# Four small changes of order and place in a two-layer transformer kernel: last addition, score buffer, a square root, a value tile

## The chip, the cores and the metric

The kernel runs on one core of a Trainium2 chip as one program. The metric is device time in microseconds (us). The core has a matrix engine (TensorE, PE in the profile, its weight loads PEld), VectorE (DVE), ScalarE (ACT), GpSimd (POOL) and SyncE (SP), which here only issues transfers. Each engine takes its instructions in the order of its own program and waits on semaphores that the others raise. PE writes only to PSUM (`ps`, eight banks of 128x512 numbers).

## The reference, cut to what matters

Two layers over x of 1024 tokens by 256:

```python
for each layer:
    xn = layernorm(x)
    s  = attention(xn)
    g  = silu(ffn(xn))
    x  = x + s * g
```

The second attention has 16 query heads and 4 key/value heads of width 128. It works on 1024 tokens in a causal way:

```python
scores = q @ k.T + alibi            # alibi: slope * distance
scores = 30.0 * tanh(scores / sqrt(128) / 30.0)
probs  = softmax(causal(scores));  ctx = probs @ v
```

The second ffn routes each token to 4 of 32 experts, plus one shared expert:

```python
logits = flat @ router_w.T
scores = sqrt(softplus(logits))
_, idx = top_k(scores + expert_bias, 4)
```

Precision is kept by splitting each operand of a product in a high and a low part (`_hi`, `_lo`); three matmuls (lines 516 to 518 of the profile, the helper `mm3`) make one product.

## The kernel before, in words

**Order.** All semaphores and orders are written by hand. For the second layer `schedule()` writes one list of steps, and `follow(engine)` makes from it the list of each engine. The steps are: `project(n, half)` (one q or k head for 512 tokens), `values(t)` (the value tile of 128 tokens), `scores(h, j)` (scores of head h with key tile j against all later queries, (8-j)*128 wide), `context(h, t)`, `turn` (transposing the context), `out` (projecting it), and the router's small parts. A score row has the number n = 8*h + j; this text calls it row n, and there are 128 of them. `context` of head h-1 runs beside the scores of head h. A table `ROUTER` says behind which score row each router part stands, for ACT and DVE apart; the DVE parts are numbered 0 to 9 up to the biased router score.

**A score row.** PE makes row n in one of two PSUM halves (n % 2). It waits that DVE has read row n-2 (`s1_bias`). DVE adds the distance term and writes the sum to `cap` (L1509). ACT takes tanh in place (L1160) and exp from there into `P1` (L1165), and POOL masks the diagonal tile of `P1` (L1738). `cap` has two slots of 1024, used in turn. DVE may write row n once ACT's exp of row n-2 is done (`s1_exp`).

**Start of the heads.** `project` goes PE, DVE (products with cos and sin, L1497 and L1499), POOL (their sum, L1845), ACT (the high part, L1154), POOL (the low part, L1853). Row 0 needs the low part of the second half of head 0's q. `values` is made by PE and copied from PSUM by DVE (L1480).

**Router.** sqrt(softplus) is computed with Exp, Ln and Sqrt on ACT (parts 0, 1, 2 of ACT, L1178, L1181 and L1184) and one Newton step on DVE behind each (for the square root, DVE parts 6 to 8, L1565 to L1570). ACT loads another function table when it goes from Exp or Tanh to Ln or Sqrt and back.

**End.** For each token tile t DVE adds pairs of expert rows (L1713), PE sums them (L952), ACT takes silu (L1230, `mix1_a`), DVE multiplies with `s_tok` (L1723, `mix1_b`), POOL adds the product to `x_tok` (L1882), and SP sends the tile out (L508). `mix1_a` and `mix1_b` have two slots each; DVE's loop makes the pairs of tile t and then the product of tile t-2. The names in the profile leave buffer numbers out: `P` is `P1`, `yp`/`gu` hold the pair sums, `mix_b` is `mix1_b`, `scr` is any of the router's scratch rows.

Of the kernel before, what the change touches and what calls it, by code (L numbers as in the profile page):

```python
# [7 lines left out]
ALU = mybir.AluOpType  # L8
ACT = mybir.ActivationFunctionType
# [7 lines left out]
P = 128  # L17
TOK = 1024
NT = TOK // P
# [78 lines left out]
H1, G1, D1 = 16, 4, 128  # L98
REP = H1 // G1
CAP = 30.0  # L100
# [12 lines left out]
NO_ROW = 1 << 20  # L113


OFF = [sum((NT - i) * P for i in range(j)) for j in range(NT + 1)]
TRI = OFF[NT]

# [35 lines left out]
def build_program(nc, x_in, wqkv_in, wout_in, lns_in, lnb_in, packed_in, scales_in,  # L154
# [5 lines left out]
    with ExitStack() as ctx:  # L160
        def sem(name):
            return ctx.enter_context(nc.semaphore(name))

        def alloc(scope):
            return lambda name, shape, dt=F32: scope.enter_context(nc.sbuf_tensor(name, shape, dt))


        sb = alloc(ctx)
        ident = sb("ident", [P, P])
        x_tok = sb("x_tok", [P, NT, D])  # L170
# [19 lines left out]
        sb = alloc(l0)  # L190
# [21 lines left out]
        sb = alloc(l0m)  # L212
# [14 lines left out]
        sb = alloc(l0w)  # L227
# [5 lines left out]
        sb = alloc(l0w)  # L233
# [10 lines left out]
        sb = alloc(l0a)  # L244
# [25 lines left out]
        sb = alloc(l1b)  # L270
# [16 lines left out]
        mix1_b = sb("mix1_b", [P, 2, D])  # L287
# [7 lines left out]
        sb = alloc(l1a)  # L295
# [10 lines left out]
        k_lo = sb("k_lo", [P, 2, TOK], F32R)  # L306
        P1 = sb("P1", [P, 2, TRI])
        V1 = sb("V1", [P, NT, G1, D1 + 1])
        cap = sb("cap", [P, 2, TOK])
        dist = sb("dist", [P, TOK])  # L310
        rot = sb("rot", [P, 3, HALF])
        c_rden = sb("c_rden", [P, 3, 1])
# [91 lines left out]
        fT_ready, f_ps, fth_ready, x_ready = sem("fT_ready"), sem("f_ps"), sem("fth_ready"), sem("x_ready")  # L404
        table_ready = sem("table_ready")
        mixed, shift_ready = sem("mixed"), sem("shift_ready")
# [4 lines left out]
        s1_ps, s1_bias, s1_exp, s1_mask = sem("s1_ps"), sem("s1_bias"), sem("s1_exp"), sem("s1_mask")  # L411
# [101 lines left out]
        def _(pe):  # L513
# [276 lines left out]
            def context(h, t):  # L790
# [8 lines left out]
                for j in range(t + 1):  # L799
                    a = OFF[j] + (t - j) * P  # L800
                    last = pe.matmul(ps[:, 4 + r % 2, o:o + D1 + 1], P1[:, h % 2, a:a + P], V1[:, j, h // REP, :],  # L801
# [170 lines left out]
        def _(act):  # L972
# [71 lines left out]
            for s in range(2 * U0):  # L1044
# [10 lines left out]
                t = tile_at(s, 2)  # L1055
# [11 lines left out]
            for t in range(NT + 1):  # L1067
                if 2 <= t < NT:
                    stack_hi(t)
                if t >= 1:  # L1070
                    r = t - 1
# [21 lines left out]
            for n in range(len(UNITS0)):  # L1093
                R, heads, a, e = UNITS0[n]
                w = e - a
# [60 lines left out]
            def scores(h, j):  # L1156
                n = h * NT + j
                w = (NT - j) * P
                act.wait_ge(s1_bias, n + 1)
                act.activation(cap[:, n % 2, 0:w], cap[:, n % 2, 0:w], ACT.Tanh, scale=1.0 / (CAP * float(D1) ** 0.5))\  # L1160
                    .then_inc(act_step, 1)
                act.wait_ge(act_step, n + 1)
                if j == 0 and h >= 2:
                    act.wait_ge(c_ps, 3 * (h - 1))
                act.activation(P1[:, h % 2, OFF[j]:OFF[j] + w], cap[:, n % 2, 0:w], ACT.Exp, scale=CAP)\  # L1165
                    .then_inc(s1_exp, 1)

            def turn_part(h, half):
# [65 lines left out]
        def _(dve):  # L1234
            steps = [2]
# [164 lines left out]
            for t in range(NT + 1):  # L1400
                if 2 <= t < NT:
                    stack_lo(t)
                if t >= 1:
                    r = t - 1
# [97 lines left out]
            def scores(h, j):  # L1502
                n = h * NT + j
                w = (NT - j) * P
                dve.wait_ge(s1_ps, n + 1)
                if n >= 2:
                    dve.wait_ge(s1_exp, n - 1)
                slope = float(np.float32(2.0) ** np.float32(-(h + 1) * 8.0 / H1))
                dve.scalar_tensor_tensor(out=cap[:, n % 2, 0:w], in0=dist[:, 0:w], scalar=slope,  # L1509
                                         in1=psf[:, 1024 * (n % 2):1024 * (n % 2) + w], op0=ALU.mult, op1=ALU.add)\  # L1510
                    .then_inc(s1_bias, 1)

# [202 lines left out]
            for t in range(NT + 2):  # L1715
                if t < NT:
                    add_pairs(t)
                if t >= 2:
                    r = t - 2
                    dve.wait_ge(fth_ready, r + 1)  # L1720
                    if r >= 2:
                        dve.wait_ge(x_ready, NT + r - 1)
                    dve.tensor_tensor(mix1_b[:, r % 2, :], mix1_a[:, r % 2, :], s_tok[:, r, :], ALU.mult).then_inc(mixed, 1)  # L1723


        @block.gpsimd
        def _(pool):
            steps = [0]
# [104 lines left out]
            def scores(h, j):  # L1833
                causal(P1[:, h % 2, OFF[j]:OFF[j] + P], s1_exp, h * NT + j, s1_mask)

# [41 lines left out]

            for b in range(NBLK):
                send_y(b)
            for t in range(NT):  # L1880
                pool.wait_ge(mixed, NT + t + 1)
                pool.tensor_tensor(x_tok[:, t, :], x_tok[:, t, :], mix1_b[:, t % 2, :], ALU.add).then_inc(x_ready, 1)  # L1882

VAR_STEP = 2 * NT + 1
STACK_STEPS = (2 * U0 - 5, 2 * U0 - 3)
# [2 lines left out]
TOP_PARTS = 10  # L1888
SUM_PARTS = TOP_PARTS + 5 + TOPK
PICK_PARTS = SUM_PARTS + 6  # L1890
ROUTER = {"act": [11, 14, 28],
          "dve": [12, 20, 20, 21, 22, 23, 29, 30, 31, 31]
          + [36, 37, 38, 39, 44, 44, 45, 46, 47]
          + [52, 53, 54, 55, 60, 61]
          + [62, 63, 68, 69, 70, 71, 76, 77]
# [9 lines left out]
def schedule():  # L1905

    steps = []
    first = PROJ.index(("q", 0))
    steps += [("project", 0, 0), ("values", 0), ("values", 1), ("turn_x", 1, 1), ("project", first, 0), ("values", 2), ("values", 3)]
    steps += [("project", 0, 1), ("project", first, 1)] + [("values", t) for t in range(4, NT)]  # L1910
    for h in range(H1 + 1):

        todo = []
        if h + 1 < H1:
            at = PROJ.index(("q", h + 1))
            if h % REP == 2 and h // REP + 1 < G1:
                todo += [("project", at - 1, 1)]
            todo += [("project", at, 0), ("project", at, 1)]
            if h % REP == 1 and h // REP + 1 < G1:
                todo += [("project", at + 1, 0)]  # L1920
        if h == 0:
            todo += [("logits", 0, 0), ("logits", 0, 1), ("turn_logits", 0, 0)]
        for j in range(NT):
            if h < H1:
                steps.append(("scores", h, j))
            if h >= 1:
                steps.append(("context", h - 1, j))

            outs = [("out", (h - 2) // PAIR - 1, 1 + 2 * j + i) for i in (0, 1) if 1 + 2 * j + i < NT]
            outs = outs if h >= PAIR + 2 and (h - 2) % PAIR == 0 else []  # L1930
            steps += outs[:1]
            if todo:
                steps.append(todo.pop(0))
            steps += outs[1:]

            if h >= 2 and j in (3, 4):
                steps.append(("turn", h - 2, j - 3))
            if h >= PAIR + 1 and (h - 2) % PAIR == PAIR - 1 and j == 7:
                steps += [("out", (h - 2) // PAIR, 0)]
            if h == RANKS_AT and j == 3:  # L1940
                steps.append(("ranks", 0, 0))
    steps += [("turn", H1 - 1, 0), ("turn", H1 - 1, 1)]
    steps += [("moe", s) for s in range(MOE_EARLY)]
    return steps
# [8 lines left out]
def follow(engine):  # L1953
# [3 lines left out]
    for n, s in enumerate(STEPS1):  # L1957
# [4 lines left out]
        if name == "scores":  # L1962
            out.append(s)
            if engine in ROUTER:
                out += [("router", part) for part, at in enumerate(ROUTER[engine]) if at == NT * s[1] + s[2]]
            if engine == "pool" and NT * s[1] + s[2] in SEND_AT:
# [114 lines left out]
```

## Time and profile before

| | us |
|---|---|
| median of 3 runs | 845.72 (844.31 to 847.45) |
| the profiled execution, its own time | 846.73 |
| its span in the trace | 844.9 |
| PE / PEld busy | 787.4 / 642.0 |
| DVE / ACT / POOL busy | 605.4 / 465.3 / 429.8 |

The span is 1.8 us shorter than the execution's own time; that rest lies outside the trace. A row of the timeline has the start in us from the span's start, the duration in us, the engine, the line, the operation with output and input, the shapes and the count, and in brackets how long the engine had been idle before it and which work ended that wait. A wait is put down to the work that came last, and where an instruction waits for two things the named one can be the wrong one. In the windows view PEclk is the granted clock of TensorE: 1.00 is 2.4 GHz and 0.50 is 1.2 GHz.

### The profile page before, as it was taken

The page shows a single profiled execution, that of the slowest core. Times are in us where ns is not written, and L with a number is a line of the kernel's source. Part 1 is how long each engine was busy: PE and PEld are TensorE (multiplying, and loading weights), DVE is VectorE, ACT ScalarE, POOL GpSimd, SP SyncE. Part 2 cuts the span into 40 slices and gives each one's busy share as a digit, 9 for nine tenths or more (in the row PEclk, how much of TensorE's full clock was granted, in tenths as well). Part 3 has the DMA queues.
Part 4 walks back from the last instruction along what each step waited for, and adds up shares of the span by engine and source line. Part 5 has one row for each costly group of instructions (what it writes and reads, how often), then busy time and mean ns, then how long its engine had stood idle before and what let it go on. Part 6 is the DMA issues. An engine that isn't in the chain of part 4 may idle for free.

```text
span 844.9 us, 14053 instructions
## 1 busy us (share of the span) xinstructions
PE 787.4 (93%) x4927; PEld 642.0 (76%) x4927; DVE 605.4 (72%) x1069; ACT 465.3 (55%) x822; POOL 429.8 (51%) x487
## 2 busy tenths in 40 slices
PE   7999999998888988899899999999999999999993
PEld 6776776774333376798798899889989999888881
DVE  8588868658999787789788688986777544445544
ACT  4433342379888643786665566556656725555421
POOL 1767837423555455455245435757565415555423
PEclk9999999999999999999999999999999999999997
DMA  5211195000000040000000000101011887543134
GB/s 184 76 38 38 38 288 145 1 1 1 1 1 2 16 132 13 20 11 22 7 19 7 26 7 20 51 25 58 18 46 33 240 303 268 165 133 101 27 101 149
DMA packets 50117, 59.82 MB, mean 71 GB/s; under 512 B 13560, under 2 KB 41085, under 8 KB 50049
## 3 DMA queue, kind: packets, MB, share of 16 engines
q1 hardware_dynamic: 45488, 50.49, 19.4%
q0 software_dynamic: 4560, 8.44, 2.8%
q8 instruction: 41, 0.67, 0.3%
q14 instruction: 28, 0.22, 0.1%
HBM read 41.11 MB, written 21.86 MB: 75 GB/s over the span
## 4 chain that ended last, share of the span: by engine, by line
PE 55%; DVE 9%; ACT 7%; POOL 7%; issue 5%; DMA 1%; SPq 0%; POOLq 0%; ACTq 0%; DVEq 0%
PE ps L801 12%; PE ps L516 8%; PE ps L518 8%; PE ps L517 8%; PE ps L894 4%; PE ps L891 3%; PE ps L925 3%; POOL A L1814 2%; DVE cap L1509 2%; PE ps L712 2%; POOL rot L1845 2%; PE ps L873 1%; PE ps L558 1%; ACT A L1108 1%; DVE swap L1499 1%
## 5 line engine op out<-in xcount | busy, mean ns | idle before, releaser
L801 PE MATMUL ps<-V,P 128*128 128x129 f32 x1152 | 150.7, 276 | 0.0
L1160 ACT ACTIVATE cap<-cap 128x1024 f32<-128x1024 f32 (+7 forms) x128 | 87.1, 681 | 113.7 <-DVE cap L1509 108.1
L801 PEld LDWEIGHTS ps<-V,P 128*128 128x128 f32 x1152 | 143.3, 192 | 2.7
L1509 DVE SCALAR_TENSOR_TENSOR cap<-dist,ps 128x1024 f32<-128x1024 f32 (+7 forms) x128 | 95.4, 750 | 27.9 <-PE ps L518 20.4
L1738 POOL TENSOR_SCALAR_AFFINE_SELECT P<-P 128x128 f32<-128x128 f32 x128 | 39.0, 305 | 144.4 <-ACT P L1165 143.8
L1870 POOL DMA_INDIRECT y_scratch<-y_sb,aux_s x63 | 62.2, 987 | 63.9 <-ACT y_sb L1205 33.7
L1165 ACT ACTIVATE P<-cap 128x1024 f32<-128x1024 f32 (+7 forms) x128 | 87.7, 685 | 4.1
L516 PE MATMUL ps<-q_hi,k_hi 128*128 128x512 f32 x192 | 71.9, 374 | 7.4 <-DVE cap L1509 5.9
L518 PE MATMUL ps<-q_lo,k_hi 128*128 128x512 f32 x192 | 66.9, 348 | 0.0
L517 PE MATMUL ps<-q_hi,k_lo 128*128 128x512 f32 x192 | 66.5, 346 | 0.0
L516 PE MATMUL ps<-xT_hi,w_hi 128*128 128x512 f32 x128 | 56.4, 441 | 2.9 <-POOL w_lo L1758 1.9
L1665 DVE TENSOR_SCALAR gu<-ps 128x256 f32<-128x256 f32 (+1 forms) x63 | 28.9, 458 | 41.0 <-PE ps L894 16.2
L1845 POOL TENSOR_TENSOR rot<-rot,swap 128x512 f32<-128x512 f32 x40 | 51.9, 1298 | 9.7 <-DVE swap L1499 9.6
L1499 DVE TENSOR_TENSOR swap<-ps,sin 64x512 f32<-64x512 f32 x80 | 55.1, 689 | 1.1
L1049 ACT ACTIVATE e_g<-ps 128x512 f32<-128x512 f32 x32 | 19.1, 597 | 66.4 <-PE ps L518 66.4
L1436 DVE TENSOR_TENSOR A<-A 128x1024 f32<-128x1024 f32 (+2 forms) x40 | 49.6, 1287 | 4.5 <-ACT A L1108 4.5
L518 PE MATMUL ps<-xT_lo,w_hi 128*128 128x512 f32 x128 | 50.6, 396 | 0.0
L517 PE MATMUL ps<-xT_hi,w_lo 128*128 128x512 f32 x128 | 50.4, 394 | 0.0
L1197 ACT ACTIVATE sg<-gu 128x128 f32<-128x128 f32 (+1 forms) x63 | 20.4, 323 | 53.3 <-DVE gu L1665 35.7
L1108 ACT ACTIVATE A<-ps 128x1024 f32<-128x1024 f32 (+2 forms) x48 | 43.5, 966 | 7.5 <-PE ps L608 7.5
L516 PEld LDWEIGHTS ps<-q_hi,k_hi 128*128 128x128 f32 x192 | 36.3, 189 | 13.4 <-DVE cap L1509 5.2
L1853 POOL TENSOR_TENSOR q_lo<-rot,q_hi 128x512 fp32r<-128x512 f32 x32 | 41.2, 1287 | 9.1 <-ACT q_hi L1154 8.9
(293 smaller groups left out, 2097.4 us busy)
## 6 DMA issues: line engine op xcount, KB each, us to landing
xg_scratch<-blank SPq DMA_DIRECT2D x1, 8127.0 KB, 31.3
xa<-xg_scratch SPq DMA_DIRECT2D x63, 128.0 KB
ew<-in_experts SPq DMA_DIRECT2D x3, 1920.0 KB, 10.0
y<-y_scratch SPq DMA_DIRECT2D x8, 512.0 KB
pk<-in_packed SPq DMA_DIRECT2D x8, 384.0 KB, 3.1
pks<-in_scales SPq DMA_DIRECT2D x8, 384.0 KB, 4.2
ew<-in_experts SPq DMA_DIRECT2D x1, 3072.0 KB
wqk<-in_wqk SPq DMA_DIRECT2D x20, 128.0 KB
```

Of the source, the lines that this page charges most:

```text
L516: pe.matmul(o, l_hi, r_hi, start=start, stop=False)
L517: pe.matmul(o, l_lo, r_hi, start=False, stop=False)
L518: return pe.matmul(o, l_hi, r_lo, start=False, stop=stop)
L801: last = pe.matmul(ps[:, 4 + r % 2, o:o + D1 + 1], P1[:, h % 2, a:a + P], V1[:, j, h // REP, :], start=(j == 0), stop=(j == t))
L1108: act.activation(dst, src, ACT.Square).then_inc(s0_sq, 1)
L1160: act.activation(cap[:, n % 2, 0:w], cap[:, n % 2, 0:w], ACT.Tanh, scale=1.0 / (CAP * float(D1) ** 0.5))\
L1165: act.activation(P1[:, h % 2, OFF[j]:OFF[j] + w], cap[:, n % 2, 0:w], ACT.Exp, scale=CAP)\
L1436: dve.tensor_tensor(a, a, a, ALU.mult).then_inc(s0_four, 1)
L1499: last = dve.tensor_tensor(swap[to, i % 2, :], b[frm, :], sin1[frm, tk], ALU.mult)
L1509: dve.scalar_tensor_tensor(out=cap[:, n % 2, 0:w], in0=dist[:, 0:w], scalar=slope, in1=psf[:, 1024 * (n % 2):1024 * (n % 2) + w], op0=ALU. ...
L1845: pool.tensor_tensor(r, r, swap[:, i % 2, :], ALU.add).then_inc(pj_rot, 1)
L1870: pool.indirect_dma_start(out=y_dram, out_offset=bass.IndirectOffsetOnAxis(ap=aux_s[:, b, 0:1].bitcast(U32), axis=0), in_=y_sb[:, b % YRIN ...
```

## The change

Four edits.

- The last addition, `x_tok += mix1_b`, is issued by DVE behind its product of the same tile, with a wait on that product; POOL's eight additions are gone.
- `cap` is one flat piece of 2048, and each row of a head has a fixed place in it, `CAP_AT[j]`. Rows 2 and 3 of a head still wait for the exp of row n-2; all others wait for that of row n-3.
- The square root of the router stands behind row 22 instead of row 28 on ACT, and seven of the first ten DVE parts stand one or two rows sooner.
- `values(3)` comes behind `project(.., 1)` of k head 0 and q head 0 instead of ahead of them.

```diff
+CAP_AT = (0, 1024, 0, 1280, 768, 0, 1280, 1920)
...
-        cap = sb("cap", [P, 2, TOK])
+        cap = sb("cap", [P, 2 * TOK])
...
-                act.activation(cap[:, n % 2, 0:w], cap[:, n % 2, 0:w], ACT.Tanh, scale=1.0 / (CAP * float(D1) ** 0.5))\
+                act.activation(cap[:, CAP_AT[j]:CAP_AT[j] + w], cap[:, CAP_AT[j]:CAP_AT[j] + w], ACT.Tanh, scale=1.0 / (CAP * float(D1) ** 0.5))\
...
-                if n >= 2:
-                    dve.wait_ge(s1_exp, n - 1)
+                free = n - 1 if j in (2, 3) else n - 2
+                if free >= 1:
+                    dve.wait_ge(s1_exp, free)
...
                     dve.tensor_tensor(mix1_b[:, r % 2, :], mix1_a[:, r % 2, :], s_tok[:, r, :], ALU.mult).then_inc(mixed, 1)
+                    dve.wait_ge(mixed, NT + r + 1)
+                    dve.tensor_tensor(x_tok[:, r, :], x_tok[:, r, :], mix1_b[:, r % 2, :], ALU.add).then_inc(x_ready, 1)
...
-            for t in range(NT):
-                pool.wait_ge(mixed, NT + t + 1)
-                pool.tensor_tensor(x_tok[:, t, :], x_tok[:, t, :], mix1_b[:, t % 2, :], ALU.add).then_inc(x_ready, 1)
...
-ROUTER = {"act": [11, 14, 28],
-          "dve": [12, 20, 20, 21, 22, 23, 29, 30, 31, 31]
+ROUTER = {"act": [11, 14, 22],
+          "dve": [12, 19, 20, 20, 21, 21, 28, 29, 30, 31]
...
-    steps += [("project", 0, 0), ("values", 0), ("values", 1), ("turn_x", 1, 1), ("project", first, 0), ("values", 2), ("values", 3)]
-    steps += [("project", 0, 1), ("project", first, 1)] + [("values", t) for t in range(4, NT)]
+    steps += [("project", 0, 0), ("values", 0), ("values", 1), ("turn_x", 1, 1), ("project", first, 0), ("values", 2)]
+    steps += [("project", 0, 1), ("project", first, 1)] + [("values", t) for t in range(3, NT)]
```

On DVE at the start of the second layer, the value copies (`V<-ps`) and the two projections of the second query half stand before like this:

```order
L1480 COPY V<-ps 128x4x128 [waits v_ps] x2
L1497 TENSOR_TENSOR rot<-ps,cos 128x512 [waits pj_rot,pj_ps]
L1499 TENSOR_TENSOR swap<-ps,sin 64x512 x2
L1497 TENSOR_TENSOR rot<-ps,cos 128x512 [waits pj_rot,parts_ready,pj_ps]
L1499 TENSOR_TENSOR swap<-ps,sin 64x512 x2
L1480 COPY V<-ps 128x4x128 [waits v_ps] x4
```

And now:

```order
L1481 COPY V<-ps 128x4x128 [waits v_ps]
L1498 TENSOR_TENSOR rot<-ps,cos 128x512 [waits pj_rot,pj_ps]
L1500 TENSOR_TENSOR swap<-ps,sin 64x512 x2
L1498 TENSOR_TENSOR rot<-ps,cos 128x512 [waits pj_rot,parts_ready,pj_ps]
L1500 TENSOR_TENSOR swap<-ps,sin 64x512 x2
L1481 COPY V<-ps 128x4x128 [waits v_ps] x5
```

One copy of four moved behind the projections; PE's value tile moved with it.

On ACT, in head 3, rows 27 to 29 (640, 512 and 384 wide) before, with the router's square root (`scr`):

```order
L1165 ACTIVATE P<-cap 128x512 [waits act_step]
L1184 ACT_TABLE_LOAD
L1184 ACTIVATE scr<-scr 128x256 [waits sp_b]
L1172 ACTIVATE cT_hi<-ps 128x512 [waits cT_ps]
L1160 ACT_TABLE_LOAD
L1160 ACTIVATE cap<-cap 128x384 [waits s1_bias]
```

Now it stands at the end of head 2, between row 22 (256 wide) and row 23 (128 wide):

```order
L1166 ACTIVATE P<-cap 128x256 [waits act_step]
L1185 ACT_TABLE_LOAD
L1185 ACTIVATE scr<-scr 128x256 [waits sp_b]
L1161 ACT_TABLE_LOAD
L1161 ACTIVATE cap<-cap 128x128 [waits s1_bias]
L1166 ACTIVATE P<-cap 128x128 [waits act_step]
L1161 ACTIVATE cap<-cap 128x1024 [waits s1_bias]
```

The two table loads and the square root moved as one piece, six rows ahead.

On DVE, in head 2 behind the `cap` of row 20 (512 wide), before:

```order
L1509 SCALAR_TENSOR_TENSOR cap<-dist,ps 128x512 [waits s1_exp,s1_ps]
L1550 TENSOR_SCALAR scr<-scr 128x256 [waits sp_a]
L1551 TENSOR_TENSOR scr<-scr 128x256 [waits vec]
L1553 TENSOR_TENSOR scr<-scr 128x256 [waits vec]
L1530 TENSOR_TENSOR cT_lo<-ps,cT_hi 128x512 [waits cT_hi_ready,vec]
L1509 SCALAR_TENSOR_TENSOR cap<-dist,ps 128x384 [waits s1_exp,s1_ps]
L1555 RECIPROCAL scr<-scr 128x256
L1530 TENSOR_TENSOR cT_lo<-ps,cT_hi 128x512 [waits cT_hi_ready,vec]
```

And now, up to the same second `cT_lo`:

```order
L1552 TENSOR_SCALAR scr<-scr 128x256 [waits sp_a]
L1553 TENSOR_TENSOR scr<-scr 128x256 [waits vec]
L1511 SCALAR_TENSOR_TENSOR cap<-dist,ps 128x512 [waits s1_exp,s1_ps,vec]
L1555 TENSOR_TENSOR scr<-scr 128x256
L1557 RECIPROCAL scr<-scr 128x256 [waits vec]
L1532 TENSOR_TENSOR cT_lo<-ps,cT_hi 128x512 [waits cT_hi_ready,vec]
L1511 SCALAR_TENSOR_TENSOR cap<-dist,ps 128x384 [waits s1_exp,s1_ps]
L1559 TENSOR_TENSOR scr<-scr 128x256
L1560 TENSOR_TENSOR scr<-scr 128x256 [waits vec]
L1562 TENSOR_SCALAR scr<-scr 128x256 [waits vec]
L1563 TENSOR_TENSOR scr<-scr 128x256 [waits vec]
L1532 TENSOR_TENSOR cT_lo<-ps,cT_hi 128x512 [waits cT_hi_ready]
```

The first two router instructions moved ahead of row 20's `cap`, the reciprocal ahead of row 21's, and four more (L1557 to L1561 of before) ahead of row 22's.

## Rows read from the trace of the kernel before

**Rows 1.** The page, part 1: busy us, share of the span, instructions.
```profile
PE 787.4 (93%) x4927; PEld 642.0 (76%) x4927; DVE 605.4 (72%) x1069; ACT 465.3 (55%) x822; POOL 429.8 (51%) x487
```

**Rows 2.** Waits of PE from 310 to 690 us: total, times, longest.
```profile
PE ps L516 <- DVE cap L1509: 5.9, 7, 1.5
```

**Rows 3.** Timeline, rows 4 to 8 of the scores, heads 0 and 1.
```profile
343.79 0.35 PE L518 MATMUL ps<-q_lo,k_hi 128*128 128x384 f32 x1
344.52 0.74 ACT L1165 ACTIVATE P<-cap 128x640 f32<-128x640 f32 x1
345.36 0.55 DVE L1509 SCALAR_TENSOR_TENSOR cap<-dist,ps 128x384 f32<-128x384 f32 x1 [1.49 <-ACT P L1165]
...
345.97 0.33 PE L516 MATMUL ps<-q_hi,k_hi 128*128 128x128 f32 x1 [1.48 <-DVE cap L1509]
...
346.54 0.42 DVE L1509 SCALAR_TENSOR_TENSOR cap<-dist,ps 128x256 f32<-128x256 f32 x1 [0.63 <-PE ps L518]
...
347.11 0.47 PE L516 MATMUL ps<-q_hi,k_hi 128*128 128x512 f32 x1 [0.59 <-DVE cap L1509]
...
349.42 1.22 DVE L1509 SCALAR_TENSOR_TENSOR cap<-dist,ps 128x1024 f32<-128x1024 f32 x1 [0.96 <-PE ps L518]
```

**Rows 4.** Windows: length, busy us of PE, PEld, DVE, ACT, POOL, PEclk, DMA.
```profile
348.00:350.00 2.00, 2.00 (x7) 1.66 (x6) 1.01 (x3) 0.68 (x3) 0.68 (x2) 0.50 0.11 37
350.00:352.00 2.00, 2.00 (x8) 1.55 (x7) 0.68 (x2) 1.29 (x2) 0.00 (x0) 0.69 0.00 0
...
347.50:348.00 0.50, 0.50 (x4) 0.39 (x3) 0.49 (x2) 0.47 (x2) 0.27 (x1) 0.84 0.92 303
...
405.00:420.00 15.00, 12.44 (x81) 10.96 (x81) 11.90 (x23) 8.74 (x14) 2.75 (x6) 1.00 0.03 9
```

**Rows 5.** Timeline, projections and values ahead of row 0.
```profile
320.16 1.29 DVE L1480 COPY V<-ps 128x512 f32<-128x512 f32 x2
...
324.15 1.29 POOL L1845 TENSOR_TENSOR rot<-rot,swap 128x512 f32<-128x512 f32 x1 [0.60 <-DVE swap L1499]
...
331.46 0.50 PE L516 MATMUL ps<-q_hi,k_hi 128*128 128x512 f32 x1 [1.35 <-POOL q_lo L1853]
```

**Rows 6.** Timeline, heads 2 and 3: router parts, their neighbours, PE's gaps.
```profile
382.23 1.38 DVE L1551 TENSOR_TENSOR scr<-scr 128x256 f32<-128x256 f32 x1
385.96 1.75 DVE L1555 RECIPROCAL scr<-scr 128x256 f32<-128x256 f32 x1
389.35 0.42 DVE L1557 TENSOR_TENSOR scr<-scr 128x256 f32<-128x256 f32 x1
...
389.58 0.47 PE L516 MATMUL ps<-q_hi,k_hi 128*128 128x512 f32 x1 [1.10 <-DVE cap L1509]
...
393.00 1.06 ACT L1160 ACTIVATE cap<-cap 128x1024 f32<-128x1024 f32 x1 [1.76 <-DVE cap L1509]
...
404.08 0.69 DVE L1530 TENSOR_TENSOR cT_lo<-ps,cT_hi 128x512 fp32r<-128x512 f32 x1 [2.44 <-ACT cT_hi L1172]
...
405.25 1.28 ACT L1184 ACT_TABLE_LOAD   x1
406.54 0.42 ACT L1184 ACTIVATE scr<-scr 128x256 f32<-128x256 f32 x1
...
414.22 0.47 PE L516 MATMUL ps<-xT_hi,wqk_hi 128*128 128x512 f32 x1 [2.07 <-DVE s_tok L1538]
```

**Rows 7.** Timeline, the last tiles.
```profile
828.11 1.05 DVE L1713 TENSOR_TENSOR yp<-y 128x512 f32<-128x512 f32 x1 [0.30 <-DMA y<-y_scratch]
829.09 0.41 DVE L1723 TENSOR_TENSOR mix_b<-mix_a,s_tok 128x256 f32<-128x256 f32 x1
831.11 0.68 DVE L1713 TENSOR_TENSOR gu<-y 128x512 f32<-128x512 f32 x1
835.14 0.86 DVE L1723 TENSOR_TENSOR mix_b<-mix_a,s_tok 128x256 f32<-128x256 f32 x1 [0.69 <-POOL x_tok L1882]
...
836.08 0.72 POOL L1882 TENSOR_TENSOR x_tok<-x_tok,mix_b 128x256 f32<-128x256 f32 x1 [0.36 <-DVE mix_b L1723]
```

More of the change, by code:

```diff
@@ L1164, in scores @@
                     act.wait_ge(c_ps, 3 * (h - 1))
-                act.activation(P1[:, h % 2, OFF[j]:OFF[j] + w], cap[:, n % 2, 0:w], ACT.Exp, scale=CAP)\
+                act.activation(P1[:, h % 2, OFF[j]:OFF[j] + w], cap[:, CAP_AT[j]:CAP_AT[j] + w], ACT.Exp, scale=CAP)\
                     .then_inc(s1_exp, 1)
@@ L1505, in scores @@
                 dve.wait_ge(s1_ps, n + 1)
-                if n >= 2:
-                    dve.wait_ge(s1_exp, n - 1)
+                free = n - 1 if j in (2, 3) else n - 2
+                if free >= 1:
+                    dve.wait_ge(s1_exp, free)
                 slope = float(np.float32(2.0) ** np.float32(-(h + 1) * 8.0 / H1))
-                dve.scalar_tensor_tensor(out=cap[:, n % 2, 0:w], in0=dist[:, 0:w], scalar=slope,
+                dve.scalar_tensor_tensor(out=cap[:, CAP_AT[j]:CAP_AT[j] + w], in0=dist[:, 0:w], scalar=slope,
                                          in1=psf[:, 1024 * (n % 2):1024 * (n % 2) + w], op0=ALU.mult, op1=ALU.add)\
```

## The prediction

> **What bounds the kernel now.** I read the busy shares first: PE is busy 93% of the span and no other engine above 72% [rows 1]. So a change pays where PE stands idle or runs at the low clock, or behind PE's last work. Then I listed PE's waits in the attention of the second layer, where three of the four edits lie. The largest is on DVE's bias step: 5.9 us in 7 waits [rows 2]. After that I went through the timeline, gap by gap. Four places touch the edits.
>
> First, between heads 0 and 1. DVE has nothing to do for 1.49 us before row 5's bias at 345.36, because that buffer still holds row 3, whose exp ends at 344.52 + 0.74 = 345.26. PE waits 1.48 us for it with row 7, and 0.59 us more for row 6's bias with row 8 [rows 3]. Right behind these two gaps the granted clock falls: 0.84 in 347.5 to 348, 0.50 in 348 to 350, 0.69 in the mean of 350 to 352 [rows 4]. These are the levels 1.2 and 2.4 GHz.
>
> Second, PE's wait of 1.35 us for row 0, on POOL's low part of q [rows 5]. Third, gaps of 1.10 us ahead of row 24 and of 2.07 us behind head 3 [rows 6]. Fourth, the end, where DVE, PE, ACT, DVE and POOL follow one another per tile [rows 7].
>
> **The change, part by part.** Times are those of the profiled execution.
>
> *The places in `cap`.* Row 5 now waits for the exp of row 2, long done, so only for PE: its matmuls end at 343.79 + 0.35 = 344.14. The bias takes 0.55 and ends at 344.7; PE starts row 7 at 344.8 instead of 345.97. Row 6 waits for row 3's exp (345.26) instead of row 4's, takes 0.42 and ends at 345.7. (Its wait is put down to PE in the trace, but PE had ended row 6 long before.) Row 8 starts at 345.8 instead of 347.11: 1.3 us sooner [rows 3]. From there to 386 the timeline has no gap on PE, so this stays. PE's gaps there shrink to about 0.3 and 0.4 us, and I expect the clock not to fall. The low stretch: 0.16 of 0.5 below full speed means 0.16 us; then 2 us at half, then 0.31 of 2 lost; the lost time is 0.08 + 1.00 + 0.62 = 1.7 us [rows 4]. PE is busy in all of it and DVE waits for it (0.96 us ahead of row 8's bias [rows 3]), so it is on the path. Together 3.0 us. Bounds: 1.3 if the clock falls anyway, 3.2 if row 8 starts with no gap at all. In later heads I found no gap of PE that this wait makes: 0.
>
> *The value tile.* DVE copies two value tiles in 1.29 us at 320.16; one of them, 0.65, now comes behind the projections. POOL's sum of the next projection, which waited 0.60 us for DVE's products, starts that much sooner [rows 5], behind its own work. The rest of the line to row 0 is POOL and ACT work back to back, so row 0 starts 0.6 us sooner, at 330.85. PE reaches it at about 330, since the value tile that it makes later only fills a wait of its own. Bounds: 0 (another value copy in the way) to 0.65. I take 0.6.
>
> *The router's square root.* It helps head 3 and costs head 2. In head 2 two instructions come ahead of row 20's bias; with POOL at work beside them they are slow (the second 1.38 us against 0.42 for its like without [rows 6]). A reciprocal of 1.75 us comes ahead of row 21's, and four more of about 0.42, with POOL beside them for a time, ahead of row 22's. Of these, a part is only exchanged with what stood there. Going through DVE's list, the bias of row 21 ends 0.9 us later (a wait for ACT's `cT_hi` hides part of the reciprocal), that of row 22 1.1 to 1.7 us later. PE starts row 24 1.1 to 1.7 later than 389.58. On ACT the piece of 1.28 + 0.42 + 1.28 = 3.0 us stands ahead of row 23. ACT has 1.76 us idle before row 24 [rows 6]; with row 22 late as well, row 24's exp ends 2.2 to 2.8 us later. What is queued behind it: POOL's mask of row 24, then POOL's sum for the next q, ACT's `cT_hi`, and DVE, which waited 2.44 us for `cT_hi` at 404.08 and will now get it 1.5 to 2.1 us later. Against that, ACT loses the 3.0 us behind row 28, and DVE its wait for the square root. With the reciprocal now ahead of the second `cT_lo`, DVE's addition that PE waits for at 414.22 comes 0.1 to 0.7 us sooner. PE is up to 1.7 later but had a gap of 2.07 us before that point, which absorbs it. I take 0.2 gained; bounds: a loss of 1.0 (the lateness of row 24 kept) and a gain of 2.1 (that gap gone, nothing lost).
>
> In this case's trace a table load takes 1.28 us and the function starts at once (405.25 + 1.28 = 406.53, then 406.54) [rows 6]. The Trainium skill, page "ScalarE: Activation LUTs", section "What ACT_TABLE_LOAD costs", adds a drain of about 1.38 us to each switch. By that rule the piece would hold ACT by 2.8 us more, and moving it to where row 24 is due would lose more than I count; the trace shows no such drain, so the sum goes without it.
>
> *The last addition.* Without POOL beside it, a pair sum takes 0.68 and a product 0.41; beside POOL's additions the first takes 1.05 and the last product 0.86 [rows 7]. An addition on DVE has the shape of the product: 0.42, and about 0.05 for its wait on the product. So DVE needs 0.68 + 0.41 + 0.42 + 0.05, less overlaps, 1.5 us a tile, about what it needs now. From 828.15 (the pairs of tile 4, held by the transfer) four tiles bring the pairs of tile 7 to an end at 833.25, as before. The two tiles before the last take 1.75 us of DVE meanwhile. PE's sum (1.13) and silu (0.38) give 834.85; product and addition end at 835.75. Before, POOL ended at 836.08 + 0.72 = 836.80 [rows 7]. Gain 1.05; I take 1.0. The eight transfers behind go on as before, since only issue and landing of the last one follow. Bounds: 0.4 (the two tiles before stand in the way) to 1.3.
>
> The rows show that two-input work on VectorE and GpSimd's hold each other up. By the Trainium skill, page "GPSIMD Engine Reference", section "1. Specifications", GpSimd shares its SBUF interfaces with VectorE when that has two SBUF inputs; the trace agrees with 0.86 against 0.41. Without such sharing DVE would need 1.1 us a tile before and 1.5 after, and the edit would gain next to nothing.
>
> *Sum.* 3.0 + 0.6 + 0.2 + 1.0 = 4.8 us, on 846.73: 841.9. That execution lies 1.0 above the median of the runs; the clock's fall may be missing in some of them, and after the change it should be missing in all. I take off 0.3 for this and say 841.6.
>
> **The rivals.** (a) The clock still falls somewhere near, since which gaps make it fall is not plain: 2.07 us behind head 3 did not (1.00 in 405 to 420 [rows 4]), 1.48 and 0.59 did. Against: the new gaps are small. Gain 4.8 - 1.7 = 3.1: 843.6. (b) The router edit pays in full: the gap of 2.07 goes and head 2's lateness vanishes in it. For: DVE loses its wait for the square root. Against: `cT_hi` comes late. Gain 4.6 + 2.1 = 6.7: 840.0. (c) The `cap` edit does not free PE, because DVE waits for something that the trace hides behind the exp: gain 1.8, 845.0. (d) Slower: ACT's queue becomes the bound from row 22 on. Its 3.0 us are not made up, the line POOL, ACT, DVE to `cT_lo` is late by that much in each of heads 3 to 5, and PE waits for it each time. Three heads at 3.0 are 9.0 us lost: 846.7 - 4.6 + 9.0 = 851.1. It decides from 8.8 us lost, the 4.6 of the other edits and the 4.2 of half a per cent; below that the sum is no change. Against: ACT is busy 55% of the span [rows 1].
>
> **How the numbers follow.** Forecast (4.2 to 5.6 gained) 0.57, (a) 0.17, (b) 0.14, (c) 0.07, (d) 0.05. A measurement of this kernel tells about 0.5% from no change, 4.2 us, that is below 841.5. The forecast lies on that line: 0.28 of its chance below, 0.29 within. Faster 0.28 + 0.14 = 0.42; same 0.29 + 0.17 + 0.07 = 0.53; slower 0.05. The range leaves (d) and the outer half of (c) out: 839.0 to 845.2.
>
> **What would show it.** Row 5's bias starts 0.1 us behind PE's last matmul of row 5; clock 1.00 throughout 344 to 354; row 0 at 330.85; row 24 on PE about 2 us (not 3.6) sooner than before; the gap behind head 3 at 0.3 to 0.8 us; DVE's last addition ending 1.0 us closer to the pairs of tile 4. It would be wrong if the clock is at 0.50 anywhere between heads 0 and 4, or if PE's gap behind head 3 stays above 2 us.

## The result: 9 us faster, most of it where no term of the forecast lay

The changed kernel takes 836.01 us (median of 4 runs, 833.08 to 838.65) against 845.01 (844.3 to 847.45) of the kernel before: ratio 0.9886, interval 0.9864 to 0.9908. The forecast was 841.6 and its range ended at 839.0. The profiled execution took 838.65, its span 836.9.

The page of the kernel after, part 1, answers to [rows 1]:

```profile
PE 790.9 (95%) x4927; PEld 645.2 (77%) x4927; DVE 607.8 (73%) x1077; ACT 466.2 (56%) x822; POOL 424.0 (51%) x479
```

The eight additions have gone from POOL (487 to 479 instructions) to DVE (1069 to 1077). Busy times hardly move. The largest move is behind PE's last work, in rows that I had not listed. First the kernel before, the queue rows of its closing line and SyncE's waits (total, times, longest):

```profile
L160 ACTq DRAIN  x1: 414/414/414, 834.5 to 834.5; - x1
L160 DVEq DRAIN  x1: 872/872/872, 835.2 to 835.2; - x1
L160 POOLq DRAIN  x1: 8607/8607/8607, 836.0 to 836.0; - x1
...
SPq L160 <- PEq L160: 6.1, 1, 6.1
SPq L160 <- DMA out<-x_tok: 1.4, 1, 1.4
```

Then the kernel after:

```profile
L161 DVEq DRAIN  x1: 464/464/464, 834.4 to 834.4; - x1
L161 POOLq DRAIN  x1: 9497/9497/9497, 812.9 to 812.9; - x1
...
SPq L161 <- DMA out<-x_tok: 1.4, 1, 1.4
SPq L161 <- PEq L161: 0.2, 1, 0.2
```

A row reads: line, engine's queue, instruction, duration in ns (least, median, most), first and last start in us. At the end of the program the trace has a DRAIN row for every engine. For ACT and DVE it takes 0.4 to 0.9 us. POOL's drain takes 8607 ns, and before the change it began at 836.0, with the last addition; it ended at 844.6, and the span at 844.9. SyncE had seen the last output land and then waited 6.1 us more for the other engines. In the kernel after POOL's last work is an indirect DMA, the drain begins at 812.9 and is over at 822.4, beside the tail. SyncE's wait is 0.2 us. (The wait is put down to PE's queue; by the drain rows it is POOL's.)

Of the timeline after, the rows that answer to [rows 3]:

```profile
346.18 0.34 PE L519 MATMUL ps<-q_lo,k_hi 128*128 128x384 f32 x1
...
346.55 0.56 DVE L1511 SCALAR_TENSOR_TENSOR cap<-dist,ps 128x384 f32<-128x384 f32 x1 [0.29 <-PE ps L519]
...
346.59 0.28 PE L519 MATMUL ps<-q_lo,k_hi 128*128 128x256 f32 x1
...
346.92 0.74 ACT L1166 ACTIVATE P<-cap 128x640 f32<-128x640 f32 x1
...
347.16 0.33 PE L517 MATMUL ps<-q_hi,k_hi 128*128 128x128 f32 x1 [0.30 <-DVE cap L1511]
...
347.76 0.42 DVE L1511 SCALAR_TENSOR_TENSOR cap<-dist,ps 128x256 f32<-128x256 f32 x1 [0.65 <-PE ps L519]
...
348.33 0.58 PE L517 MATMUL ps<-q_hi,k_hi 128*128 128x512 f32 x1 [0.61 <-DVE cap L1511]
```

Row 5's bias starts 0.03 us behind PE's last matmul of that row (346.52), and PE's gap ahead of row 7 is 0.30 instead of 1.48. The gap ahead of row 8 is still 0.61. Row 6's bias starts at 347.76, right behind ACT's exp of row 3 (346.92 + 0.74 = 347.66), as forecast; the trace puts the wait down to PE, but PE had ended row 6 at 346.87. From row 0 to row 8 it is 348.33 - 333.86 = 14.47 us, before 347.11 - 331.46 = 15.65 [rows 3, 5]: 1.2 us. Windows after (columns as in [rows 4]):

```profile
348.00:350.00 2.00, 1.67 (x5) 1.32 (x6) 1.10 (x4) 1.94 (x5) 0.67 (x4) 0.64 0.37 95
350.00:352.00 2.00, 2.00 (x7) 1.72 (x6) 0.93 (x1) 1.05 (x4) 0.76 (x3) 0.51 0.30 102
...
392.00:394.00 2.00, 1.75 (x6) 1.38 (x7) 0.81 (x4) 1.81 (x3) 0.29 (x1) 0.73 0.02 5
394.00:396.00 2.00, 2.00 (x7) 1.71 (x6) 1.22 (x1) 1.97 (x3) 0.00 (x0) 0.50 0.00 0
```

The clock goes down to its lower level all the same (0.51 in 350 to 352), and once more at 392 to 396, where it didn't before. The prediction had named 0.50 between heads 0 and 4 as a sign of being wrong. This text calls such a stretch at the lower clock a fall. Row 0 and heads 2 and 3, answering to [rows 5, 6]:

```profile
333.86 0.50 PE L517 MATMUL ps<-q_hi,k_hi 128*128 128x512 f32 x1 [0.56 <-POOL q_lo L1857]
...
388.01 0.33 PE L517 MATMUL ps<-q_hi,k_hi 128*128 128x128 f32 x1 [1.30 <-DVE cap L1511]
...
392.25 0.47 PE L517 MATMUL ps<-q_hi,k_hi 128*128 128x512 f32 x1 [1.85 <-DVE cap L1511]
...
393.03 1.28 ACT L1185 ACT_TABLE_LOAD   x1
394.32 0.42 ACT L1185 ACTIVATE scr<-scr 128x256 f32<-128x256 f32 x1
...
408.39 0.69 DVE L1532 TENSOR_TENSOR cT_lo<-ps,cT_hi 128x512 fp32r<-128x512 f32 x1 [2.53 <-ACT cT_hi L1173]
...
415.95 0.47 PE L517 MATMUL ps<-xT_hi,wqk_hi 128*128 128x512 f32 x1 [0.30 <-DVE s_tok L1540]
```

PE's wait for row 0 is down from 1.35 to 0.56. The gap ahead of row 24 has grown from 1.10 to 1.85, the one behind head 3 has shrunk from 2.07 to 0.30. The tail, answering to [rows 7]:

```profile
830.16 0.69 DVE L1715 TENSOR_TENSOR gu<-y 128x512 f32<-128x512 f32 x1
830.77 0.42 DVE L1725 TENSOR_TENSOR mix_b<-mix_a,s_tok 128x256 f32<-128x256 f32 x1
831.22 0.43 DVE L1727 TENSOR_TENSOR x_tok<-x_tok,mix_b 128x256 f32<-128x256 f32 x1
...
833.89 0.42 DVE L1725 TENSOR_TENSOR mix_b<-mix_a,s_tok 128x256 f32<-128x256 f32 x1
834.35 0.42 DVE L1727 TENSOR_TENSOR x_tok<-x_tok,mix_b 128x256 f32<-128x256 f32 x1
```

A tile takes DVE 0.69 + 0.42 + 0.43 less overlaps, 1.4 us, and nothing is stretched (no 1.05 and no 0.86). The last addition ends at 834.77; the span ends 2.1 us later. Before, it ended at 836.80 and the span 8.1 later.

Where the 8.0 us between the two spans are, point by point (after less before, each time from the span's start): row 0 +2.40, row 8 +1.22, row 24 +2.67, behind head 3 +1.73, the last gate-and-up step 808.45 - 809.03 = -0.58, last addition -2.03, end of span -8.0. So 6.0 lie behind the last addition. Up to row 0 the profile after had lost 2.4, in code that mostly isn't changed (its clock had also fallen once in layer 0, 0.50 in 227 to 229, and that of before had not). In the mixture stage, unchanged too, it won 2.2 (from DVE's first read of a gate-and-up product to the start of its last 512-wide one, 109.54 against 111.77). Both needed a control.

### The profile page after: what moved, and what is told of

Same layout as the page of the kernel before. It is cut to its first block, busy times and chain, and to the rows that moved or that the text cites. A ratio compares the mean times of both kernels' runs of the same rounds, so it can differ in the third digit from the quotient of the medians.

```text
span 836.9 us, 14053 instructions
## 1 busy us (share of the span) xinstructions
PE 790.9 (95%) x4927; PEld 645.2 (77%) x4927; DVE 607.8 (73%) x1077; ACT 466.2 (56%) x822; POOL 424.0 (51%) x479
## 4 chain that ended last, share of the span: by engine, by line
PE 54%; DVE 11%; POOL 6%; ACT 6%; issue 4%; DMA 3%; SPq 0%; POOLq 0%; ACTq 0%; DVEq 0%
PE ps L802 12%; PE ps L517 8%; PE ps L519 8%; PE ps L518 8%; PE ps L895 4%; PE ps L926 3%; PE ps L892 3%; POOL A L1818 2%; DVE cap L1511 2%; DVE swap L1500 2%; PE ps L713 2%; PE ps L874 1%; DMA xa<-xg_scratch 1%; PE ps L559 1%; ACT A L1109 1%
## 5 line engine op out<-in xcount | busy, mean ns | idle before, releaser
L1161 ACT ACTIVATE cap<-cap 128x1024 f32<-128x1024 f32 (+7 forms) x128 | 87.3, 682 | 112.4 <-DVE cap L1511 106.9
```

The lines of the kernel that those rows point to most:

```text
L1161: act.activation(cap[:, CAP_AT[j]:CAP_AT[j] + w], cap[:, CAP_AT[j]:CAP_AT[j] + w], ACT.Tanh, scale=1.0 / (CAP * float(D1) ** 0.5))\
```

## The experiments

**One edit at a time**, each on the kernel before. The four shared one chip and a before of 848.38 us.

The last addition alone:

```diff
+                    dve.wait_ge(mixed, NT + r + 1)
+                    dve.tensor_tensor(x_tok[:, r, :], x_tok[:, r, :], mix1_b[:, r % 2, :], ALU.add).then_inc(x_ready, 1)
...
-            for t in range(NT):
-                pool.wait_ge(mixed, NT + t + 1)
-                pool.tensor_tensor(x_tok[:, t, :], x_tok[:, t, :], mix1_b[:, t % 2, :], ALU.add).then_inc(x_ready, 1)
```

> The kernel before with one edit, the last addition on DVE. Theory 1 (the closing drain of POOL, 8.6 us long in the trace of before, starts only behind POOL's last addition and is what the end of the program waits for; with no addition on POOL it starts at the last scatter and is hidden): 6 us less at the barrier and 1 us less in the tail, 837.5 to 839 on a median of 845 before, POOL's drain starting near its last scatter, and the span ending about 2 us behind the last addition. Theory 2 (only the chain in the tail is shorter, as predicted; the rest of the gain is from the other edits or from the mixture stage): 844, drain still at the end. Theory 3 (the whole difference is luck with the clock): no change.

Measured: 840.41 us, ratio 0.9914 (0.9885 to 0.9942), which is 7.3 us (4.9 to 9.8). Its closing rows:

```profile
L160 POOLq DRAIN  x1: 9493/9493/9493, 816.1 to 816.1; - x1
...
SPq L160 <- PEq L160: 0.2, 1, 0.2
```

This edit alone brings the larger part of the gain.

The places in `cap` alone:

```diff
+CAP_AT = (0, 1024, 0, 1280, 768, 0, 1280, 1920)
...
-                if n >= 2:
-                    dve.wait_ge(s1_exp, n - 1)
+                free = n - 1 if j in (2, 3) else n - 2
+                if free >= 1:
+                    dve.wait_ge(s1_exp, free)
```

> The kernel before with one edit, the fixed places in cap and the later wait. As predicted: PE starts row 8 1.2 to 1.3 us sooner; 843.7 if the clock falls behind heads 0 and 1 as often as before, 842 if it then never falls there. Rival: the wait is replaced by another, no change.

Measured: 845.5 us, 0.9971 (0.9956 to 0.9986), 2.5 us (1.2 to 3.7). Row 0 to row 8 takes 347.49 - 333.03 = 14.46 us, and here the clock stayed up behind it. The closing wait is 6.1.

The router's square root alone:

```diff
-ROUTER = {"act": [11, 14, 28],
-          "dve": [12, 20, 20, 21, 22, 23, 29, 30, 31, 31]
+ROUTER = {"act": [11, 14, 22],
+          "dve": [12, 19, 20, 20, 21, 21, 28, 29, 30, 31]
```

> The kernel before with one edit, the router's square root and first DVE parts sooner. Prediction: 0.2 us less (+1.0 to -2.1). The trace of the changed kernel speaks for a loss: PE reached row 24 1.4 us later, the clock fell right behind that gap, and the gap behind head 3 shrank to 0.3 us, so 0 to +1. The gap ahead of row 24 should be above 1.5 us and the one behind head 3 below 0.7.

Measured: 846.3 us, 0.998 (0.996 to 1.0): up to 3.4 us gained or nothing. Gaps of 1.30 and 1.85 us ahead of rows 23 and 24, 0.30 behind head 3, and the clock down right behind row 24.

The value tile alone (`("values", 3)` moved behind the two second projections):

> The kernel before with one edit, the fourth value tile behind the second query half. Prediction: row 0 starts 0.6 us sooner and the run is 0.6 us shorter. Rival: the value copies now stand in the way, 0.

Measured: 847.71 us, 0.9997 (0.998 to 1.0013). The timing can't tell it from nothing. In the trace the wait ahead of row 0 is 0.54 instead of 1.35.

**The addition against the rest, and what its place costs.** The next three shared another chip, with a before of 845.3 us. First the changed kernel with the additions back on GpSimd:

```diff
-                    dve.wait_ge(mixed, NT + r + 1)
-                    dve.tensor_tensor(x_tok[:, r, :], x_tok[:, r, :], mix1_b[:, r % 2, :], ALU.add).then_inc(x_ready, 1)
...
+            for t in range(NT):
+                pool.wait_ge(mixed, NT + t + 1)
+                pool.tensor_tensor(x_tok[:, t, :], x_tok[:, t, :], mix1_b[:, t % 2, :], ALU.add).then_inc(x_ready, 1)
```

> The changed kernel with the last addition back on POOL (three edits left). Theory 1 (drain): it loses 6 to 7 us against the changed kernel, 842 to 843.5, with SP waiting some 6 us for the barrier at the end. Theory 2 (the gain lies in the attention and mixture stages): 837 to 838.

Measured: 842.0 us, 0.9959 (0.9944 to 0.9974). The other three edits bring 3.5 us together, and the closing wait is back:

```profile
L161 POOLq DRAIN  x1: 8608/8608/8608, 832.3 to 832.3; - x1
...
SPq L161 <- PEq L161: 6.1, 1, 6.1
```

Then the changed kernel, all additions on VectorE, with one small instruction on GpSimd behind VectorE's last product:

```diff
+            pool.wait_ge(mixed, 2 * NT)
+            pool.memset(moe_pad[:, 0:1], 0.0)
```

> The changed kernel, all additions on DVE, and one more instruction on POOL: a memset of one number per partition in an unused tile, behind a wait on DVE's last product. Theory 1: POOL's drain starts behind it at about 834 and takes its 8 to 9 us in the open, 6 to 7 us longer than the changed kernel, 842 to 843. Rival (the drain is long only behind additions that use POOL's read path, or what helped was the shorter tail): as the changed kernel, 836.

Measured: 841.96 us (837.4 to 843.98), 0.9951 (0.9936 to 0.9967). Nothing else of the computation or the tail is changed (first pair sum to end of last addition 14.76 us, as with the addition on DVE), and 5.5 us of the gain are gone (0.9951 against the changed kernel's 0.9886):

```profile
831.47 0.10 POOL L1885 MEMSET moe_pad<- 128x1 f32 x1 [19.55 <-DVE mix_b L1725]
```

```profile
L161 POOLq DRAIN  x1: 7948/7948/7948, 831.5 to 831.5; - x1
...
SPq L161 <- PEq L161: 5.8, 1, 5.8
```

An instruction of 0.10 us costs 5.5 us (as much against the next run, on the same chip and without it: 841.96 - 836.51), and 5.8 - 0.2 = 5.6 in SyncE's closing wait. That shows that neither the length of the additions nor VectorE's speed made the surprise: it is the place of POOL's last instruction.

The changed kernel with the router's tables as before (the diff of the third run, reversed):

> The changed kernel without the router edit. If that edit costs 0 to 1 us, 835 to 836; if it gains the 0.2 that was predicted, 836.2; if it gains 2, 838. The two gaps of before (1.10 ahead of row 24, about 2 behind head 3) should be back.

Measured: 836.51 us (833.62 to 837.79), 0.9893 (0.9873 to 0.9913). Against the changed kernel's 0.9886 the router edit gains 0.6 us, well inside the two intervals, so the timing can't tell its sign.

**Is it a fixed drain, and what do the clock and the controls say?** Four runs on a third chip, with a before of 845.05 us. The small write again, 4.6 us earlier:

```diff
+            pool.wait_ge(mixed, NT + 4)
+            pool.memset(moe_pad[:, 0:1], 0.0)
```

> The changed kernel, and GpSimd writes one column of zeros (0.1 us) into a buffer that nothing reads any more, 4.6 us before VectorE's last product instead of right behind it (as in the run where that small write stood behind the last product: the write at 831.5, span 839.6, 5.8 us of SyncE's wait for the other engines at the end). Theory DRAIN: what costs is the time from GpSimd's last work to the end of its closing drain, a fixed 8.1 us, as far as it isn't covered. Then SyncE's closing wait falls from 5.8 to about 1.2 us, and the kernel takes 1.0 us more than the changed one (0.9987 to 0.9999 of it). Rival TOUCH: any GpSimd work behind the waits of the tail makes the full 6 us, wherever it stands; then the wait stays at 5.8 and the time 5 to 6 us above the changed kernel. Rival NOISE: the small write itself costs nothing and the first such run was slow for its clock; then no difference from the changed kernel and a closing wait of 0.2.

Measured: 836.79 us (835.4 to 838.38), 0.9902 (0.9881 to 0.9922), 1.4 us above the control of the changed kernel on the same chip (0.9885). The intervals overlap, so the time alone doesn't show the 1.0 us that was expected; the closing rows do:

```profile
826.86 0.10 POOL L1885 MEMSET moe_pad<- 128x1 f32 x1 [14.91 <-DVE mix_b L1725]
```

```profile
L161 POOLq DRAIN  x1: 7948/7948/7948, 826.8 to 826.8; - x1
...
SPq L161 <- PEq L161: 1.2, 1, 1.2
```

The wait is 1.2 us, the number of theory DRAIN; TOUCH asked for 5.8, NOISE for 0.2. In these traces the drain ends 7.8 to 7.9 us behind the end of POOL's last work, whatever that is: an addition (836.80, drain to 844.6), the write (831.57 to 839.4, and 826.96 to 834.7), an indirect DMA (813.58 + 0.99 = 814.57 to 822.4). What is not covered by other work is lost.

TensorE kept busy in the two gaps, with a filler that changes no result:

```diff
+                for _ in range({23: 11, 24: 16}.get(n, 0)):
+                    pe.matmul(ps[:, 3, 400:HALF], x_tok[:, 0, 0:P], x_tok[:, 0, 0:HALF - 400], start=True, stop=True)
```

> The changed kernel, and TensorE runs 11 extra 128x112 matmuls ahead of row 23 and 16 ahead of row 24 (about 0.117 us each, 1.3 and 1.9 us together, into a PSUM bank that is free there), as long as its two gaps in front of them were. They leave nothing out and change no result. Theory GAPS: the clock falls behind row 24 because of the two gaps of 1.30 and 1.85 us that the router's earlier square root makes; with TensorE busy the fall at 391 to 395 is gone, rows 23 and 24 start where they did (within 0.3 us), the stretch from row 8 to the projection behind head 3 takes about 1.7 us less than with the fall (some 65.5 to 66 with none of the falls, 67.5 where only row 8's is there), and the gap of that head stays at 0.3. In the time 1 to 1.7 us less than the changed kernel. Rival OTHER: the fall comes from somewhere else (it stays), or another one follows elsewhere (as the falls of the first layer, which come and go from program to program); then the time is that of the changed kernel within 1 us. Rival LATE: the extra matmuls outlast the gaps and push rows 23 and 24 back; then slower by up to 1 us.

Measured: 835.06 us (832.87 to 836.87), 0.988 (0.9859 to 0.9901), no difference from the control.

```profile
383.30 2.61 PE L779 MATMUL ps<-x_tok 128*128 128x112 f32 x22
385.67 0.30 PE L517 MATMUL ps<-q_hi,k_hi 128*128 128x128 f32 x1
...
386.04 2.00 PE L804 MATMUL ps<-V,P 128*128 128x129 f32 x16
387.87 3.72 PE L779 MATMUL ps<-x_tok 128*128 128x112 f32 x32
391.37 0.47 PE L517 MATMUL ps<-q_hi,k_hi 128*128 128x512 f32 x1
```

Each filler is two instructions (x22 for 11, x32 for 16), so my filling was twice as long as the gaps. Rival LATE holds in the trace: row 8 to the projection behind head 3 takes 66.83 us, and the kernel isn't slower for it. The clock is 1.00 there, and four of its six runs show a granted clock of 1.000 for the whole span.

The two controls, the kernel before and the changed kernel:

> The kernel before, unchanged, as a control beside the changed one on the same chip. Ratio 1.000 within 0.001. It tells what a second profile of it shows: SyncE's closing wait 6.1 us and GpSimd's drain 8.6 us again. Open question is the mixture stage, whose first to last gate-and-up step took 111.8 us before and 109.5 after in the first two profiles, in a stretch that the change doesn't touch. Theory CHIP: it differs between chips and runs, 109 to 112.4 with no relation to the program; then the two controls agree within 0.5 us. Theory PROGRAM: it belongs to the program, and this one takes about 2 us more than the changed kernel's control.

> The changed kernel again, as a control beside the kernel before on the same chip. Sum of the parts as the earlier runs measured them: 6.0 us for the drain that is now covered, 1.0 us shorter tail, 0.8 us of the value tile, 1.3 us from row 8's earlier start and, where the clock stays up there, 1.7 more, and 0.4 lost by the router's square root: 8.7 to 10.4 us, ratio 0.9877 to 0.9897. Closing wait 0.2 us, drain hidden, a clock fall behind row 24 (391 to 395) again; at row 8 the fall may be there or not, since it was there in two of five profiles with these places in cap.

Measured: before 846.3 us, 1.0015 (1.0002 to 1.0027); after 834.87 us (832.93 to 837.52), 0.9885 (0.9861 to 0.9908), the same as the first result. The control of before is the same program as what it is compared with, and it read 1.3 us slower with an interval that leaves 1 out. So a difference of about 1 us between two timings tells nothing here by itself.

Of the mixture stage theory CHIP holds: 109.09 us (before) and 109.03 (after) on this chip, though the first pair of profiles had 111.77 and 109.54. On the first chip of the experiments the same unchanged stage took 111.2 to 112.4, on the second 109.0 to 110.0. So the 2.2 us between the first two profiles are not the change's. The head start of layer 0 isn't either: with the attention's first gap of 1.1 us on `xa` as the mark, 308.38 and 308.80 here. From that mark to row 0 the control of before takes 332.57 - 308.38 = 24.19, that of after 332.36 - 308.80 = 23.56: the value tile's 0.6 us.

The changed kernel's control missed one expectation: the fall behind row 24 was not there. Its rows at that place, from the timeline, and behind it a window:

```profile
384.94 0.33 PE L517 MATMUL ps<-q_hi,k_hi 128*128 128x128 f32 x1 [1.30 <-DVE cap L1511]
...
389.18 0.47 PE L517 MATMUL ps<-q_hi,k_hi 128*128 128x512 f32 x1 [1.85 <-DVE cap L1511]
...
411.27 0.47 PE L517 MATMUL ps<-xT_hi,wqk_hi 128*128 128x512 f32 x1 [0.32 <-DVE s_tok L1540]
```

```profile
390.00:392.00 2.00, 2.00 (x11) 1.68 (x10) 1.16 (x1) 1.97 (x3) 0.29 (x1) 1.00 0.00 0
```

The same gaps, the full clock. That gives the missing field of a table, from row 8's first matmul to the projection behind head 3, in us, one number for each profile that falls in a field:

| | clock stays up | falls at row 8 only | falls at row 24 only | falls at both |
|---|---|---|---|---|
| router as before | 65.53, 65.54 | 67.11, 67.09, 67.09 | | |
| router changed | 64.43 | | 65.88, 66.00 | 67.62, 67.47, 67.55 |

(Left out are the value tile's own run, in which the clock was down twice as long, and the two with a filler. The places in `cap` shift the stretch as a whole, since it begins at row 8.) Down a column the router edit wins 65.53 - 64.43 = 1.1 us. A fall costs 1.5 to 1.6. Where the edit brings a fall at row 24, it loses 0.4. The field that decides the 1.1 has one profile (64.48 with the short filler below is a second of its kind).

**The filler at the right length**, against the run with the longer one:

```diff
-                for _ in range({23: 11, 24: 16}.get(n, 0)):
+                for _ in range({23: 5, 24: 7}.get(n, 0)):
```

> The changed kernel, and 5 extra 128x112 matmuls ahead of row 23 and 7 ahead of row 24. Each runs as two passes of 0.117 us, so they fill 1.2 and 1.6 us of the gaps of 1.30 and 1.85 us, where the run with 11 and 16 of them (2.6 and 3.7 us) outlasted both gaps and put row 24 2.1 us back. They leave nothing out and change no result. Theory GAPS: the clock stays up behind row 24, as it did in every profile and in nearly all timed runs with the 11 and 16 (granted clock 1.000 in four of six), and row 24 isn't late; from row 8 to the projection behind head 3 it takes about 64.5 us, what the one profile of the changed kernel without any fall there took, against 66.8 with the long filler; the median is 2 us under that kernel's 835.06 (ratio 0.9880), some 833 us, ratio 0.985 to 0.987. Rival LUCK: the falls come and go whatever stands in the gaps, and the long filler met a quiet stretch; then falls are seen again in some of the runs (granted clock 0.992 to 0.996) and the ratio is that of the changed kernel, 0.988 to 0.989.

Measured: 833.95 us, the lowest of all medians and the narrowest (832.56 to 834.38), ratio 0.9871 (0.9855 to 0.9888).

```profile
383.37 1.27 PE L779 MATMUL ps<-x_tok 128*128 128x112 f32 x10
384.83 0.33 PE L517 MATMUL ps<-q_hi,k_hi 128*128 128x128 f32 x1 [0.20 <-DVE cap L1513]
...
385.22 2.00 PE L804 MATMUL ps<-V,P 128*128 128x129 f32 x16
387.06 1.71 PE L779 MATMUL ps<-x_tok 128*128 128x112 f32 x14
389.07 0.47 PE L517 MATMUL ps<-q_hi,k_hi 128*128 128x512 f32 x1 [0.30 <-DVE cap L1513]
```

The clock stays up and row 24 isn't late: the stretch takes 411.18 - 346.70 = 64.48 us, as expected (64.5). The ratio lies on the edge between the two theories, and its interval overlaps the changed kernel's, so that it is faster than the changed kernel is likely and not shown. The granted clocks, which count a fall anywhere in the span, speak for GAPS: with a filler 9 of 10 runs have 0.998 or more for the span (the tenth 0.997), the changed kernel without one in 3 of its 10 (the others 0.992 to 0.997).

## Why the prediction was wrong

**The last addition** is the step that failed. It said "The eight transfers behind go on as before, since only issue and landing of the last one follow", and it counted as gain only the 1.0 us by which the last addition ends sooner. Before the change, 8.1 us lay between that end and the end of the span, and issue and landing fill only 2.1 of them: so much remains when POOL stops early (834.77 to 836.9; 829.41 to 831.5 in the control). The other 6.0 were POOL's drain. I had read 8.1 us of end as fixed, without asking which engine ends last and what it does there, although the closing rows of before show the drain and SyncE's wait of 6.1. So the term of 1.0 measures 7.3 by itself (4.9 to 9.8). What it said of the additions themselves was right: no stretch beside POOL, 1.4 us a tile where I worked out 1.5. From the first pair sum to the end of the last addition it is 14.27 to 14.96 us in the eight profiles with DVE adding and 15.74 to 16.79 in the six with POOL, means 14.7 and 16.1, a gain of 1.4 against 1.0. By the Trainium skill, page "GPSIMD Engine Reference", section "1. Specifications", the two engines share their interfaces to SBUF; the last product of 0.42 where it was 0.86 agrees.

With 6.0 more the forecast would have been 835.6; measured are 836.0. That the rest fits to 0.4 us is in part luck. For the profiled execution the same sum is 841.9 - 6.0 = 835.9, and it took 838.65: the 1.7 us of the clock were not gained, 3.0 more were lost ahead of row 0, and 2.2 were won in the mixture stage, none of which the forecast had.

**The places in `cap`**, 3.0 forecast. The 1.3 us of earlier start measured 1.2. The 1.7 of the clock were wrong in their certainty: the forecast said of the fall that "after the change it should be missing in all", and the clock fell at row 8 in three of nine profiles with these places (the first one among them) and in four of five without. A fall costs 1.6 us, as worked out from [rows 4] within 0.1. The mean gain is then about 1.2 + (0.8 - 0.33) x 1.6 = 2.0; timed alone it was 2.5. Four of five against three of nine is too few to show that the places make the fall rarer. The timed runs point the same way (mean granted clock 0.9935 over the 12 with this edit alone, 0.9914 over the 29 of before on that chip), but the value tile alone, which leaves both waits in place, has 0.9899, so that isn't proof either. Rival (a) had this mechanism right, in some runs.

**The value tile**, 0.6 forecast: 0.6 in the traces, below what timing tells.

**The router**, 0.2 forecast with bounds of -1.0 and 2.1. Row 24 came 392.25 - 348.33 less 389.58 - 347.11 [rows 3, 6] = 1.45 us later (I had 1.1 to 1.7), and the gap behind head 3 is 0.30 (0.3 to 0.8). With the full clock the sum is a gain of 1.1, since PE's path behind row 24 is 2.55 us shorter (22.09 against 24.64 in the runs without falls): about 1.75 of it at the gap of 2.07, which is down to 0.3, and 0.8 ahead of it, mostly at a gap of 0.37 ahead of the output projection, which is gone. What I had not counted is that the two grown gaps bring the clock down: behind row 24 in five of six profiles with them, in none of six without. In the timed runs this doesn't show: the mean granted clock with the router edit alone is 0.9926 over 12, that of before 0.9914 over 29. So what the edit costs in the clock on average stays open.

The table load behaves as before the change: 393.03 + 1.28 = 394.31, and the function starts at 394.32. The drain that the Trainium skill adds to a table switch (page "ScalarE: Activation LUTs", section "What ACT_TABLE_LOAD costs") is again not in the trace.

**Rivals.** (b) named 840.0 with the router paying in full; it pays half of that, in part of the runs. (c) and (d) did not happen: PE was freed, and ACT's queue held nobody for long. No rival lay outside the four edits' own places, so none could reach 836.

The parts as measured: 6.0 drain, 1.4 tail, 0.6 value tile, 1.2 row 8, together 9.2. To this the clock and the router add between -0.4 (a fall at row 24 and none spared at row 8) and 2.7 (1.6 spared at row 8, 1.1 of the router). The medians say 9.0 (845.01 - 836.01). In the control the ratio of 0.9885 makes 9.7, the medians 10.2 (845.05 - 834.87).

What stays open: what POOL's drain does in its 7.8 us, and what decides whether the clock falls behind the same gaps (1.30 and 1.85 us with 2.0 us of work between them in both cases).

## What to carry to other kernels

Read the end of the span as a stage of its own: take the end of each engine's last work and the drain row behind it, and ask which drain the program waits for. Where GpSimd works last, as in the kernel before, its 7.8 us are on the path whatever the length of that work, less the 2 us or so that the outputs take to land anyway. A gap of PE that a move makes has two prices, its own length and a possible fall of the clock; count the second as a chance seen in several profiles, never as certain from one.

## What the runs showed of the hardware

- GpSimd's closing drain ends 7.8 to 7.9 us behind its last instruction in all 14 profiles, after additions, a 128x1 memset and indirect DMAs alike. The drains of ScalarE and VectorE at the same place take 0.4 to 0.9 us.
- A fall of TensorE's clock from 2.4 to 1.2 GHz cost 1.5 to 1.6 us each time in the attention (table above). Behind PE's gap of 2.07 us (head 3) none followed in six profiles; behind 1.30 and 1.85 us one did in five of six.
- An f32 matmul of 128x112 on plain operands is two instructions of 0.12 us each (2.61 us for 22).
- A stage of 110 us that no edit touches took 108.9 to 112.4 us. On one chip the kernel before and the changed one took the same (109.09 and 109.03), so the difference isn't the program's.
